# Interleaving the last image's output stage with the first projections of the attention, in a two-block image kernel

## The reference

```python
x = x + _L0_conv_ref(_gn(x), ...)   # group norm, then a four-direction selective scan
x = x + _L1_conv_ref(_gn(x), ...)   # group norm, then attention: 12 heads of 32, rotary, relative bias
```

```python
mu = y.mean(-1, keepdims=True)
var = y.var(-1, keepdims=True)
y = (y - mu) / jnp.sqrt(var + 1e-05) * out_norm_g + out_norm_b
y = y * jax.nn.silu(z)
return y @ out_proj_w.T
```

## Time and profile before

| | |
|---|---|
| median of 3 runs | 3094.7 us (3093.93 to 3096.32) |
| the profiled execution: its time | 3094.16 us |
| its span from first to last instruction | 3092.4 us |
| busy share of the span: PE, DVE, ACT, POOL | 87%, 73%, 52%, 44% |
| last matmul of image 3's scan, start of that row | 1631.37 us |
| first scores of image 0's attention | 1737.13 us |
| mean clock granted to TensorE, share of full | 0.968 |

### The profile page before, as it was taken

The page is one execution under the profiler, slowest core; times in us unless marked ns, Lnnn a source line. Parts: engine busy times, 40 slices in busy tenths (PEclk is TensorE's granted clock), DMA queues, the critical chain, the costliest instruction groups (busy, mean ns, idle before and its releaser), DMA issues. The chain is left out here.

```text
span 3092.4 us, 40835 instructions
## 1 busy us (share of the span) xinstructions
PE 2684.6 (87%) x16088; PEld 1346.6 (44%) x16088; DVE 2242.5 (73%) x2157; ACT 1614.7 (52%) x1972; POOL 1351.2 (44%) x624
## 2 busy tenths in 40 slices
PE   5579788988889878687767999999999999999999
PEld 2134233333333333232322565555555565556555
DVE  0398988899888998899992566646665566646665
ACT  2464655555555556555541456625564356525564
POOL 1577887887778877788670200011000300011000
PEclk9799999999999999999996999999999999999999
DMA  2344544455444555445551210120120210120110
GB/s 78 108 142 129 163 150 144 150 140 168 165 145 148 142 170 167 154 160 140 197 172 36 76 36 18 39 75 1 36 56 14 63 36 22 35 76 1 35 36 22
DMA packets 93526, 297.03 MB, mean 96 GB/s; under 512 B 16172, under 2 KB 18872, under 8 KB 93208
## 3 DMA queue, kind: packets, MB, share of 16 engines
q1 hardware_dynamic: 93336, 294.43, 30.8%
HBM read 238.27 MB, written 23.07 MB: 85 GB/s over the span
## 5 line engine op out<-in xcount | busy, mean ns | idle before, releaser
L1599 POOL TENSOR_TENSOR arena<-arena 128x1024 f32<-128x1024 f32 x384 | 903.2, 2357 | 307.4 <-DVE arena L1081 297.7
L1081 DVE TENSOR_TENSOR_SCAN arena<-PS,arena 128x1024 f32<-128x1024 f32 x384 | 879.0, 2289 | 102.2 <-ACT PS L1442 70.9
L577 PE MATMUL PS<-arena,ident 128*128 128x512 f32 x1536 | 762.0, 620 | 15.0 <-ACT arena L1453 12.8
L1442 ACT ACTIVATE PS<-arena,a_inf,a_neg 128x1024 f32<-128x1024 f32 x384 | 463.8, 1208 | 586.3 <-DVE arena L1081 580.3
L1201 DVE CUSTOM_DVE_ANT_1 arena<-PS,arena 128x1024 f32<-128x1024 f32 x384 | 467.7, 1219 | 323.4 <-PE PS L880 321.8
L1526 ACT ACTIVATE arena<-arena,neg_max 128x1024 f32<-128x1024 f32 x384 | 441.0, 1148 | 494.8 <-DVE neg_max L1201 494.8
L1089 DVE TENSOR_TENSOR arena<-arena,PS 128x1024 f32<-128x1024 f32 x384 | 460.8, 1200 | 57.7 <-PE PS L568 56.4
L568 PE MATMUL PS<-arena,sel 96*128 96x512 bf16 x768 | 239.4, 394 | 295.5 <-DVE arena L1089 291.7
L1629 POOL TENSOR_TENSOR arena<-arena 128x512 f32<-128x512 f32 x48 | 68.4, 1425 | 955.2 <-ACT arena L1495 955.2
L880 PE MATMUL PS<-arena 64*128 64x512 f32 x1536 | 431.6, 640 | 19.3 <-DMA arena<-arena 12.8
L577 PEld LDWEIGHTS PS<-arena,ident 128*128 128x128 f32 x1536 | 302.5, 198 | 275.0 <-issue 221.4
(11 more groups left out here) (125 smaller groups left out, 2205.3 us busy)
## 6 DMA issues: line engine op xcount, KB each, us to landing
arena<-b_rows SPq DMA_DIRECT2D x256, 512.0 KB, 3.7
arena<-b_rows SPq DMA_DIRECT2D x256, 256.0 KB, 3.9
arena<-arena SPq DMA_DIRECT2D x192, 128.0 KB, 3.3
arena<-arena SPq DMA_DIRECT2D x120, 64.0 KB, 2.6
normed<-x_in SPq DMA_DIRECT2D x12, 512.0 KB, 5.4
residual<-x_in SPq DMA_DIRECT2D x12, 512.0 KB, 5.6
x<-residual SPq DMA_DIRECT2D x12, 512.0 KB, 5.3
xn<-residual SPq DMA_DIRECT2D x12, 512.0 KB, 4.7
```

What stands on the lines that cost most here:

```text
L577: last = pe.matmul(dst[:, half(h)], lhs, rhs[:, half(h)], start=start, stop=stop, skip_group_check=True)
L1081: dve.tensor_tensor_scan(HS[:, at % 2, ::step], DA[:, ::step], DBU[:, at % R3, ::step], 0.0, ALU.mult, ALU.add).then_inc(scan_done.sem, 1)
L1442: act.activation(DA, DELTA[:, tile % 2, :], ACT.Exp, bias=a_inf[:, col:col + 1], scale=a_neg[:, col:col + 1]).then_inc(da_ready.sem, 1)
L1599: pool.tensor_tensor(DBU[:, at % R3, :], DU[:, tile % 2, :], BSB[:, at % R3, :], ALU.mult).then_inc(dbu_ready.sem, 1)
```

## The change

The output stage of image 3 and the start of image 0's attention, up to the first scores, are written as one interleaved order on each engine: `PE_BOTH`, `DVE_BOTH`, `ACT_BOTH`. A number in these lists is a job of the attention's start (0 to 3 `proj`, 4 and 5 `rel`, 6 and 7 `relh`), a tuple a job of the output stage, `("v", t)` a block of v. No computation is added or left out. So that both can live side by side, v uses banks 2 and 3 instead of 0 to 3 for image 0, and the gate z of image 3 is loaded to other slots. SP's queue is reordered too.

```diff
-            return slot(19 + j) if m == B - 1 else ZS[:, j, :]
+            return slot(14 + j) if m == B - 1 else ZS[:, j, :]
...
+        PE_BOTH = ([0, 1, ("y", 0, 0), ("y", 0, 1), ("y", 0, 2), 2, ("y", 1, 0), ("y", 1, 1), ("y", 1, 2), 3, ("v", 0),
+                    ("var", 0), ("var", 1), ("v", 1), ("v", 2), 4, ("v", 3), ("v", 4), ("out", 0), ("out", 1), 5, ("v", 5),
+                    ("out", 2), ("out", 3), 6, ("out", 4), ("out", 5), 7, ("v", 6), ("stats",), ("v", 7)])
+        DVE_BOTH = ([0, 1, 2, 3, ("scale", 0), ("scale", 1), 4, ("add", 0), ("add", 1), 5, ("add", 2), ("add", 3), 6,
+                     ("add", 4), ("add", 5), ("add", 6), ("moments",), 7, ("var",)])
...
+        def v_bank(b, t):
+
+            return banks(t % 4 if b else 2 + t % 2, 1)
...
                 for k, (ready, count) in enumerate(((rope_ready, 2), (rope_ready, 4), (rel_saved, 2))):
+                    if b == 0 and k == 2:
+                        for part in range(CT):
+                            mid(B - 1, "x1_store", part)
                     sp.wait_ge(ready.sem, ready.after(b, count))
...
-            for job in in_order(PE_MID):
-                mid(B - 1, *job)
-            pe.wait_ge(gn2_var.sem, gn2_var.at(B))
             pe.wait_ge(att_loaded.sem, att_loaded.at(len(ATT_MATS)))
-            pe.wait_ge(onehot_loaded.sem, onehot_loaded.at(2 * HG))
...
-                    if t >= 4 and k == 0:
+                    if b == 0 and t >= 2 and k == 0:
+                        pe.wait_ge(v_saved.sem, v_saved.after(b, t - 1))
+                    elif t >= 4 and k == 0:
                         pe.wait_ge(v_saved.sem, v_saved.after(b, t - 3))
...
+                for entry in PE_BOTH if b == 0 else ():
+                    if isinstance(entry, int):
+                        if entry == 2:
+                            pe.wait_ge(y_saved.sem, y_saved.at(3 * B))
+                        job(0, entry)
+                    elif entry[0] == "v":
+                        for k in range(CT):
+                            value_product(entry[1], k)
+                    else:
+                        mid(B - 1, *entry)
+                if b == 0:
+                    pe.wait_ge(gn2_var.sem, gn2_var.at(B))
+                    pe.wait_ge(onehot_loaded.sem, onehot_loaded.at(2 * HG))
...
             for b in range(B):
                 for n in range(2 * len(PREPARED)):
+                    if b == 0 and n == 4:
+                        for job in in_order(POOL_MID):
+                            mid(B - 1, *job)
```

More of the change, by code:

```diff
@@ L369, in build @@
         JOB_AT = [{k: m for m, k in enumerate([2, 4, 6, 8, 10, 12, 16, 18, 20, 22, 24, 25, 26, 27])}, {6: 0, 10: 1}, {}]
+        PE_BOTH = ([0, 1, ("y", 0, 0), ("y", 0, 1), ("y", 0, 2), 2, ("y", 1, 0), ("y", 1, 1), ("y", 1, 2), 3, ("v", 0),
[3 more added lines that the diff above has]
+                     ("add", 4), ("add", 5), ("add", 6), ("moments",), 7, ("var",)])
+        ACT_BOTH = ([0, 1, ("yf", 0), ("sq", 0), 2, ("yf", 1), ("sq", 1), 3, ("v", 0), ("rstd",), ("v", 1), ("v", 2),
+                     ("affine", 0), ("affine", 1), ("v", 3), ("v", 4), ("v", 5), ("v", 6), ("rstd2",), ("v", 7),
+                     ("norm", 0), ("norm", 1), ("norm", 2)])
+        def v_bank(b, t):
+            return banks(t % 4 if b else 2 + t % 2, 1)
         ROPE_FOR, REL_FOR = [4, 10, 12], [2, 6, 6]
@@ L509, in _ @@
                                  ).then_inc(onehot_loaded.sem, 16)
[L510 to L515, removed]
             for b in range(B):
-                load_image(X[:, :, :], x1, b, x_loaded.sem)
+                if b:
+                    load_image(X[:, :, :], x1, b, x_loaded.sem)
                 def operands(g, j):
@@ L534, in _ @@
                             sp.dma_start(dst, src).then_inc(head_loaded[j].sem, 16)
+                if b == 0:
+                    for part in range(CT):
+                        mid(B - 1, "xn2_store", part)
+                    sp.wait_ge(x1_stored.sem, x1_stored.at(CT * B))
+                    sp.wait_ge(xn2_stored.sem, xn2_stored.at(CT * B))
+                    load_image(X[:, :, :], x1, b, x_loaded.sem)
                 for g in range(1, GROUPS):
@@ L813, in value_product @@
                         pe.wait_ge(pj_read.sem, pj_read.after(b, 0))
-                    last = pe.matmul(banks(t % 4, 1)[:, 0:C], XN[:, k, t * P:(t + 1) * P],
+                    last = pe.matmul(v_bank(b, t)[:, 0:C], XN[:, k, t * P:(t + 1) * P],
                                      W["w_qkv"][:, k, 2 * C:3 * C], start=(k == 0), stop=(k == CT - 1))
@@ L950, in project @@
                     return last
-                for m, blocks in START:
+                for entry in PE_BOTH if b == 0 else ():
[8 more added lines that the diff above has]
+                        mid(B - 1, *entry)
+                if b == 0:
+                    pe.wait_ge(gn2_var.sem, gn2_var.at(B))
+                    pe.wait_ge(onehot_loaded.sem, onehot_loaded.at(2 * HG))
+                for m, blocks in START if b else ():
                     if m is None:
@@ L1108, in _ @@
             times_c(ITEMS * B - 1)
-            for job in in_order(DVE_MID):
-                mid(B - 1, *job)
             dve.wait_ge(att_loaded.sem, att_loaded.at(len(ATT_MATS)))
@@ L1206, in biased_scores @@
                         accum_out=neg_max[:, s % 4:s % 4 + 1]).then_inc(max_done.sem, 1)
-                for m in range(len(JOBS[0])):
-                    job(0, m)
+                for entry in range(len(JOBS[0])) if b else DVE_BOTH:
+                    if isinstance(entry, int):
+                        job(0, entry)
+                    else:
+                        mid(B - 1, *entry)
                 for s in range(STEPS * GROUPS):
@@ L1475, in _ @@
             save_sums_of_pair(3 * B - 1)
-            for job in in_order(ACT_MID):
-                mid(B - 1, *job)
             for b in range(B):
@@ L1482, in save_v @@
                     act.wait_ge(v_psum.sem, v_psum.after(b, t + 1))
-                    act.activation(V[:, t, :], banks(t % 4, 1)[:, 0:C], ACT.Copy).then_inc(v_saved.sem, 1)
+                    act.activation(V[:, t, :], v_bank(b, t)[:, 0:C], ACT.Copy).then_inc(v_saved.sem, 1)
                 def job(phase, m):
@@ L1510, in save_sums @@
                                    ACT.Copy).then_inc(o_saved.sem, 1)
-                for m, blocks in START:
+                for entry in ACT_BOTH if b == 0 else ():
+                    if isinstance(entry, int):
+                        job(0, entry)
+                    elif entry[0] == "v":
+                        save_v(entry[1])
+                    else:
+                        mid(B - 1, *entry)
+                for m, blocks in START if b else ():
                     if m is not None:
@@ L1619, in _ @@
                             mid(b - 1, *job)
-            for job in in_order(POOL_MID):
-                mid(B - 1, *job)
             pool.wait_ge(att_loaded.sem, att_loaded.at(len(ATT_MATS)))
```

## The result

The changed kernel takes 3058.3 us (median of 4 runs, 3055.0 to 3060.2), the kernel before in the same comparison 3095.5: a ratio of 0.988, 95% interval 0.986 to 0.990. The forecast was 3058. The profiled execution took 3059.45 with a span of 3057.6, 34.8 us less than the span before.

What follows compares the result with a forecast made beforehand. Between image 3's scan and the first scores, engines work one at a time, PE idles and partly runs at half clock. Scores 37.9 us earlier, less 1.05 for ACT, gain 36.8: from 3094.16 to about 3058, range 3052 to 3072.

Steps and rivals of the forecast that it cites:

- The schedule of PE: From image 3's scan end to the first scores: PE's products priced one by one at full clock, 63.5 us; chance 0.60.
- The price of `rel`: Two `rel` on PE at 3.76 us each, 7.5 in all, taken from a row of 16 at 1.88.
- The covers: At each handover, PE's independent work was to outlast the other engines' path, leaving about 1.0 us of idle time.
- `proj` 2 over square and copy: In the first half, `proj` 2's 2.6 us was to cover the 2.03 us wait for square and copy.
- the gates: After `var`, the gates were to end at about 1671.9, before `out` 0 at 1673.0: cover 1.1 us.
- the sums of x: Between `out` and `stats`, DVE's 3.12 us was to be covered by 2.9 of `relh` 1 and v6; PE waits 0.2.
- The relative rows behind x1's stores: SP issues these copies after x1's third store, 6.3 us before the scores; costed at nothing, at most 2.3 us.
- The norm in front of the first exponential: ACT's three norm passes, 3.50 us, before the first exponential, 2.45 after the scores' start: 1.05 us late, counted in full.
- The clock: PE's granted clock was to stay at 1.00 from scan end to scores, with no idle gap over 0.6 us.
- A: The clock falls once at a `rel`: 2 to 4 us lost at the first, 3070 at the second; chance 0.22.
- the signs that the prediction named: For the schedule, unbroken PE work and granted clock 1.00 before the scores; against it, a window at 0.50.
- B: The clock falls early, between `y` 1 and `var`, and `out` and `rel` keep it low: at most 3099; chance 0.03.

Runs made afterwards that it cites:

- again: The changed kernel run once more with no edit, as a control; 3057.7 us, ratio 0.988.
- sp_rel_first: The changed kernel with the three stores of x1 behind the relative rows' copies in SP's queue, not in front; 3058.2 us, ratio 0.988.
- norm_late: The changed kernel with v's products between those of `rel`, and the group norm's passes behind the exponentials of steps 4, 6 and 8; 3054.5 us.
- before_warm: The kernel before the change, with 20 products that nobody reads filling PE's idle gaps behind image 3's scan; 3074.0 us, ratio 0.994.
- rel_then_out: As rel_twice, with v3 and v4 ahead of the doubled `rel` and all six `out` directly behind it; 3078.7 us, ratio 0.995.
- rel_twice: The changed kernel with the 16 products of the first `rel` done twice over; 3069.2 us, ratio 0.992.
- again2: The changed kernel with no edit, as the control of another group; 3053.8 us, ratio 0.988.
- before_out128: The kernel before the change, with the second product of each `out` of image 3 over 128 rows, not 64; 3085.3 us, ratio 0.997.
- late_out128: As norm_late, with the second product of each `out` of image 3 over 128 rows, not 64; 3051.9 us, ratio 0.987.

## Why the prediction was right

**The schedule of PE** (63.5 us of products, 64.3 in all) was right in the sum: 64.6 in every profile that has its products and no fall of the clock. That is closer than its terms were, and there luck had a part. From one start to the next in again, `rel` is 7.1 for both where 7.5 stood, and the eight blocks of v are 16.2 where 15.6 stood; `out` is 12.4 for 12.2, `proj` 10.5 for 10.3, `stats` 1.6 for 1.7, and `var` 3.7 and `y` 10.4 are as priced. The price of `rel` was read from a row with 64 columns a product, and with 32 it is a little less. That of v came from two blocks in one piece, and single blocks take up to 2.2.

**The covers** held, each of them: `proj` 2 over square and copy (0.5 us over), the gates (0.8 in again, where I had 1.1), the sums of x. PE had no wait at 1694.8, where I had 0.2, and 0.78 before the scores where I had 0.6.

**The relative rows behind x1's stores** cost nothing, as forecast; sp_rel_first shows it. The forecast's 6.3 us from their first issue to the scores doesn't follow from its own times, 1692.6 and 1699.2, which give 6.6; it was 6.5 (1694.41 to 1700.94).

**The norm in front of the first exponential**: counted at 1.05, measured 0.6 (norm_late). I had put the start of the norm and that of the scores at one moment; in fact the norm starts 0.36 earlier (1700.58 and 1700.94). The 0.6 are still there at image 1's projections, so counting it in full was right.

**The clock.** That nearly half of the gain is clock was in the sum (12 from `out`, 2.6 from `var`, 3.0 from the projections, 1.4 from `stats`, 19 in all). before_warm took 18.9 off the time, but that these two agree so well is chance: in its middle the clock gave 16.3, since the projections fell to half clock there for a while and gave 1.1. In the rivals, A's mechanism was right: the clock fell at the first `rel`, and v brought it back. It happened in the profile of the change and in none of the other three with `rel` alone, which is compatible with its chance of 0.22 and no more. There it cost 2.8 us in v and 0.6 in `rel`. By the signs that the prediction named, a window at 0.50 speaks against its own schedule, so for this one profile A was what happened. The forecast of 3058 came out better than its terms, since in this profile two things that were not counted partly cancel: the fall cost 3.4, and the scan ended 2.0 earlier. The mechanism of B, that `out` can't leave the low clock, is real too (rel_then_out). That the change is safe from it is shown for the first `rel` alone, where v3 and v4 stand between the fall and `out`; no profile had a fall at the second, which has one block of v behind it.

The sentence in which I set the Trainium skill's page "TensorE: Matmul & The Clock Gate" (Part 1: The HAM clock gate) against the trace can now be settled. The Trainium skill says there that idleness throttles and sustained activity releases. Two runs don't fit that, if an unbroken timeline of PE counts as activity: in rel_twice the clock fell from 1.00 to 0.50 in the midst of 9.41 us without idle time, and in rel_then_out it stayed at 0.50 through the 24.09 us of `out`. The same page of the Trainium skill says that the time of a weight load goes by its columns and that its rows don't matter (Part 2: What happens when you issue a matmul). For a load by itself the trace agrees: those of `w_out` took 188 ns over 128 rows and 184 over 64 in the profile of the change. All the same two groups of `out` take 3.68 with 128 rows in both and 4.27 with 128 and 64 in turn, and the runs do not say why.

The rest of the execution differs by up to 3 us between profiles of kernels that are alike there: from the first scores to the end it is 1354.0 in again2 and 1357.2 in again. The traces show where: PE waited 11.0 us for DMAs in again2 and 12.5 in again, and in again the clock was 0.53 from 2251.0 to 2254.3, behind a wait of 2.33 us for a DMA, which is 1.6 more by the rows of PE in that place (2.08 for 1.13 and 1.74 for 1.08). What stays open is why these waits differ, why `out` with 128 and 64 rows in turn is slower, and what about a matmul decides whether the clock falls or returns. The runs separate two kinds of products from the others, no more.

## What to carry to other kernels

When one stage hands its work from engine to engine and the next stage doesn't depend on it, write them as one order on each engine and check each handover by its cover, in microseconds, from rows of the profile; here that gave the stretch to 0.3 us, though its terms were off by up to 0.6 each. Look at the granted clock of such a stage first: here nearly half of what the handovers cost was in the matmuls behind them, and independent products in the gaps gave most of that back (16.3 of the 19 us counted). The fill that was tried is of 128x512 over 128 rows; thinner fill was not tried. Don't put a run of thin products in front of a run that can't bring the clock back.

## What was not expected of the hardware

- TensorE's clock fell from 2.4 to 1.2 GHz without any idle time, during 32 f32 products with 32 columns each (64 records; rel_twice, rel_then_out). With 16 such products it fell once in eight stretches, in one profile of four.
- 12 f32 products over 128 and 64 rows in turn stayed at 1.2 GHz for 24.11 and 24.09 us (before, rel_then_out). Over 128 rows in both, the clock was 0.51 in the first 5.7 us and 1.00 behind them (before_out128).
- Such a pair of products costs 2.06 us at full clock (4.12 from one start to the next for two in the profile of the change), and with 128 rows in both 1.76 (3.52 in late_out128), though that is more arithmetic.
- Short waits of PE in the attention were followed by half clock. Behind waits of 1.28 and 1.96 us for DMAs the clock was 0.50 for 3.4 us (rel_twice, 1915.7 to 1919.1); behind one of 2.33 us in again it was 0.53 from 2251.0 to 2254.3.
